# Moving the token routing and the row sends of an attention and mixture-of-experts kernel one slot later

## The reference

```python
xn = _layernorm(x, axis=-1)
x = x + attention(xn) + ffn(xn)
# attention: 16 heads of 8 numbers, causal, scores plus a decay mask, softmax, then w_proj
scores = einsum('bhqd,bhkd->bhqk', q, k) / sqrt(D) + attn_mask
y = einsum('bhqk,bhkd->bhqd', softmax(scores), v)
# ffn: 8 experts with 512 hidden numbers, the best 2 of each token
probs = softmax(einsum('btd,ed->bte', x, Wr));  topk_vals, topk_idx = top_k(probs, 2)
h = silu(einsum('btd,efd->btef', x, W1));  y = einsum('btef,edf->bted', h, W2)
out = einsum('bte,bted->btd', gate, y)
```

## Time and profile before

| | us |
|---|---|
| median of 3 runs | 507.46 (504.73 to 507.56) |
| the profiled execution: its time | 506.12 |
| the profiled execution: its span | 504.4 |
| PE busy | 478.1 |
| DVE busy | 365.7 |
| POOL busy | 366.2 |
| ACT busy | 336.6 |

### The profile page before, as it was taken

The page is one execution under the profiler, slowest core; times in us unless marked ns, Lnnn a source line. Parts: engine busy times, 40 slices in busy tenths (PEclk is TensorE's granted clock), DMA queues, the critical chain, the costliest instruction groups (busy, mean ns, idle before and its releaser), DMA issues.

```text
span 504.4 us, 13425 instructions
## 1 busy us (share of the span) xinstructions
PE 478.1 (95%) x4294; PEld 346.7 (69%) x4294; DVE 365.7 (73%) x1407; ACT 336.6 (67%) x621; POOL 366.2 (73%) x591
## 2 busy tenths in 40 slices
PE   6769899999999999999999999989999999999997
PEld 5645465555664665566566556689999999999564
DVE  7888989988999989989889897733333333333887
ACT  4789878888888888887988888752233233232762
POOL 3587987889888889889889888734454554555784
PEclk9998999999999999999999999999999999999999
DMA  6479790780470461353255153877676777672634
GB/s 188 126 278 286 201 215 16 213 199 18 133 215 28 143 182 57 122 158 102 90 159 138 51 183 112 227 223 238 199 210 208 210 208 207 191 216 69 246 118 140
DMA packets 72755, 82.24 MB, mean 163 GB/s; under 512 B 8638, under 2 KB 52704, under 8 KB 72688
## 3 DMA queue, kind: packets, MB, share of 16 engines
q1 hardware_dynamic: 68368, 72.91, 50.3%
q0 software_dynamic: 4320, 8.47, 4.7%
HBM read 49.94 MB, written 31.86 MB: 162 GB/s over the span
## 4 chain that ended last, share of the span: by engine, by line
PE 69%; DVE 17%; ACT 10%; issue 2%; DMA 1%; SPq 0%; ACTq 0%; DVEq 0%
PE psT L1498 22%; PE psT L1585 13%; PE ps L1558 12%; PE psO L1518 11%; DVE scores L1268 8%; PE ps L1470 6%; ACT probs L1008 4%; ACT scores L965 3%; PE psM L1446 2%; DVE x_all L608 2%; PE ps L1549 1%; ACT values L992 1%; DVE xt L1122 1%; DMA w_qkv<-w_attn 1%; DVE probs L1054 1%
## 5 line engine op out<-in xcount | busy, mean ns | idle before, releaser
L1268 DVE CUSTOM_DVE_ANT_0 scores<-ps,wdist 128x256 f32<-128x256 f32 (+3 forms) x512 | 217.3, 485 | 22.6 <-PE ps L1470 21.8
L1008 ACT ACTIVATE probs<-psT 128x512 f32<-128x512 f32 x320 | 173.8, 597 | 50.3 <-PE psT L1498 49.1
L875 POOL TENSOR_SCALAR scores<-scores,row_max 128x256 f32<-128x256 f32 (+3 forms) x388 | 185.3, 493 | 29.2 <-DVE row_max L1268 28.1
L1498 PE MATMUL psT<-ident,scores 128*128 128x128 f32 x1280 | 176.3, 281 | 5.7 <-ACT probs L1008 5.6
L1498 PEld LDWEIGHTS psT<-ident,scores 128*128 128x128 f32 x1280 | 137.7, 141 | 64.0 <-issue 46.3
L894 POOL DMA_INDIRECT picked_dram<-scores,row_ring x71 | 69.8, 983 | 70.0 <-DVE scores L1349 66.8
L1017 ACT ACTIVATE scores<-ps 128x512 f32<-128x512 f32 x71 | 42.3, 598 | 91.4 <-PE ps L1558 91.4
L1518 PE MATMUL psO<-probs,values 128*32 128x512 f32 (+3 forms) x1024 | 88.4, 441 | 0.0
L965 ACT ACTIVATE scores<-scores,row_max 128x512 f32<-128x512 f32 x124 | 83.0, 727 | 0.0
L1585 PE MATMUL psT<-xn_all,scores 128*128 x568 | 75.4, 276 | 1.6 <-ACT scores L1017 1.6
L1558 PE MATMUL ps<-scores,wdist 128*128 128x128 f32 x568 | 74.9, 275 | 0.6 <-DMA wdist<-w1t 0.6
(11 more groups left out here) (169 smaller groups left out, 295.3 us busy)
## 6 DMA issues: line engine op xcount, KB each, us to landing
wdist<-w1t SPq DMA_DIRECT2D x71, 256.0 KB, 3.4
k_rows<-k_dram SPq DMA_DIRECT2D x64, 96.0 KB, 3.0
q_rows<-q_dram SPq DMA_DIRECT2D x64, 96.0 KB, 2.9
row_ring<-rows_dram SPq DMA_DIRECT2D x71, 65.0 KB, 2.9
rows_dram<-row_ring SPq DMA_DIRECT2D x6, 650.0 KB, 6.3
k_dram<-k_parts SPq DMA_DIRECT2D x7, 384.0 KB, 2.4
q_dram<-q_parts SPq DMA_DIRECT2D x7, 384.0 KB, 2.6
xn_all<-picked_dram SPq DMA_DIRECT2D x4, 512.0 KB, 7.4
```

Source lines behind the costliest of these rows:

```text
L875: last = nc.gpsimd.tensor_scalar(part, part, -1.0, row_max[:, r, tile, quad:quad + 1], ALU.mult, ALU.add)
L1008: nc.scalar.activation(probs[:, at.ring(2), w, :], psT[:, w % 2], ACT.Exp, scale=-1.0).then_inc(exp_ready, 1)
L1268: last = nc.vector.tensor_tensor_reduce(out=scores[:, r, u, col:col + n], in0=bank[:, col:col + n], in1=wdist[:, at.g * QUADS + quad, SEQ ...
L1498: last = nc.tensor.transpose(psT[:, w % 2, place * P:(place + 1) * P], scores[:, at.ring(2), u, col + key * P:col + (key + 1) * P], ident[:])
```

## The change

Every entry of ROUTE moves to the next slot, so the routing stands in slots 3 to 13 in place of 2 to 12, and FIRST_SEND_SLOT is 9 in place of 8, so the sends stand in slots 9 to 28 in place of 8 to 27. SECOND_PICK_SLOT, where the second pick's places are written into the rows, follows to slot 19. The wait of R9 for the counts names slot 5, where CT now stands. Nothing is added or taken away.

```diff
-ROUTE = {2: {0: ("R1",), 1: ("R2",), 3: ("R3",)},
-         3: {0: ("R4",), 1: ("R5",), 3: ("R6",)},
-         4: {0: ("R7", "GX"), 1: ("CT",), 3: ("R8",)},
-         5: {0: ("R9",), 3: ("R10",)},
...
-         12: {0: ("R17",)}}
-FIRST_SEND_SLOT = 8
+ROUTE = {3: {0: ("R1",), 1: ("R2",), 3: ("R3",)},
+         4: {0: ("R4",), 1: ("R5",), 3: ("R6",)},
+         5: {0: ("R7", "GX"), 1: ("CT",), 3: ("R8",)},
+         6: {0: ("R9",), 3: ("R10",)},
...
+         13: {0: ("R17",)}}
+FIRST_SEND_SLOT = 9
...
-                    dve.wait_ge(misc_free, MISC["CT", 4] + 1)
+                    dve.wait_ge(misc_free, MISC["CT", 5] + 1)
```

More of the change, by code:

```diff
@@ L72 @@
 DVE_BATCHES, POOL_BATCHES = (4, 5, 6, 7), (0, 1, 2, 3)
-ROUTE = {2: {0: ("R1",), 1: ("R2",), 3: ("R3",)},
-         3: {0: ("R4",), 1: ("R5",), 3: ("R6",)},
-         4: {0: ("R7", "GX"), 1: ("CT",), 3: ("R8",)},
-         5: {0: ("R9",), 3: ("R10",)},
[L78 to L81, removed]
-         12: {0: ("R17",)}}
-FIRST_SEND_SLOT = 8
+ROUTE = {3: {0: ("R1",), 1: ("R2",), 3: ("R3",)},
+         4: {0: ("R4",), 1: ("R5",), 3: ("R6",)},
+         5: {0: ("R7", "GX"), 1: ("CT",), 3: ("R8",)},
+         6: {0: ("R9",), 3: ("R10",)},
+         7: {0: ("R11",), 3: ("R12",)},
+         8: {0: ("R13",), 3: ("R14",)},
+         9: {0: ("R15",)},
+         12: {0: ("R16",)},
+         13: {0: ("R17",)}}
+FIRST_SEND_SLOT = 9
 ALL_UNITS = UNITS * NGROUP
```

## The result

The changed kernel takes 518.32 us (median of 6 runs, 516.55 to 520.55), the kernel before 507.02 in the same comparison: a ratio of 1.0257, with an interval of 1.0226 to 1.0287 (it isn't the quotient of the two medians, which is 1.0223). By the ratio the changed kernel stands at 520.5 on that median, a little above the range of 511.5 to 520.

The account below looks back on a forecast made before the run. PE was taken to end most slots, the DVE some, and the last send's load chain to reach PE last. Early slots -0.8, sends' end +10.0 and clock +0.8 give +10.0 on 506.12; forecast 516.8 us, range 511.5 to 520.

Parts of the forecast that it names:

- The end of the sends: Hand-over to the experts: the last send starts later and PE's first up matmul moves by the whole delay, +10.0 us.
- The clock: Experts' start: after PE's idle stretch the granted clock falls to half for a while, +0.8 us, between 0 and 1.65.
- the sum of the early slots: Slots that give or receive routing, plus the XN steps: together -0.8 us, bounds about -3.5 and +3.
- The routing: Routing pieces moved one slot later: -1.0 + 0 + 1.2 + 1.0 + 0 + 0.3 us over the slots.
- Slots 2 and 6: Slot 2 loses R1 to R3, -1.0 us; slot 6 swaps R11 and R12 for R9 and R10, +1.0.
- Slot 5: It receives the counting, 2.02 us on PE, and becomes 13.2 us long with a little idle: +1.2.
- Slots 7 and 8: R13 and R14 go from slot 7 to 8; what one wins the other loses: 0, between -1 and +1.4 us.
- R16 in slot 12: Part of one term for R15 to R17, short instructions going to slots 9, 12 and 13: +0.3 us together.
- XN: Scaling of tokens on the DVE: both long cases, slots 12 and 16, become short, -2.3 us, bounds -2.4 and 0.
- rival (b): XN stays long or finds other slots, so the -2.3 falls away: 519.1 us, chance 0.13.
- Rival (a): Row tiles behind w2 issue in 1.86 us instead of 4.75, PE starts 2.9 earlier: 513.9 us, chance 0.12.
- Rival (c): Not slower: the early slots give back what the routing cost them, about 509.4 us or within 1%, chance 0.05.

Follow-up runs that it names:

- sends alone late: Kernel before with only the sends moved, to slots 9 to 28, the routing staying in slots 2 to 12: 514.57 us, ratio 1.0175.
- w1 first: Changed kernel with SP issuing four w1 ahead of its wait for the landing, then four row tiles, w2, four more row tiles: 515.22 us, ratio 1.0201.
- the kernel in which it was kept up: Changed kernel with 44 idle matmuls put in front of PE's wait for the first row tile: 521.11 us, ratio 1.0318.
- routing alone late: Changed kernel with the second pick's sends packed into slots 19 to 27, so the last send is in slot 27 as before: 509.31 us, ratio 1.0061.
- first pick's four-send slots moved, w1 first: Kernel before with those slots moved from 11 and 15 to 12 and 16, and four w1 loaded ahead of SP's wait: 508.81 us, ratio 1.0084.

## Why the prediction was right and wrong

**The end of the sends: right in its mechanism, and in its size partly by luck.** The last send starts 23.58 us into slot 27 where it was 13.50: +10.1, forecast +10.0. The prediction then kept two times of the kernel before, and both were off: from the last send to w2 it took 4.34 in place of 2.35, and w1, issued at 337.92 and used at 341.21, arrived 1.2 quicker (3.3 for 4.45). They nearly cancel; together +10.85. With the landing at 2.35 again (second pick's four-send slots moved back) the kernel is 4 us faster, 2 of them from the landing. That it was this chain is shown by the sends alone late, which have the same wait, and by w1 first, which changes only the chain.

**The clock: the size fits.** The half clock came, for longer than in the earlier trace rows. From the first up matmul to the ninth slot's the changed kernel took 0.9 us more than the kernel before, forecast 0.8, and the two other kernels with the half clock there took 0.8 and 1.5 more. That the clock alone makes this difference isn't shown: in the kernel in which it was kept up, two slower loads took as much. Behind the ninth slot the profiled execution lost another 1.2 us, 0.8 of them in two short waits near 457 us, that no part of the change explains.

**The step that failed is the sum of the early slots, -0.8.** It came out at about +1.5 (slots 2 to 28 of the profiled executions), 2.3 more than forecast, in two of its terms:

- The routing, forecast -1.0 + 0 + 1.2 + 1.0 + 0 + 0.3 = +1.5, cost +3.1 (changed kernel against sends alone late; 2.6 in the routing alone late, whose slot 6 takes 9.78). Slots 2 and 6 were right, -1.1 and +1.1. Slot 5 was +1.8 in place of +1.2; the forecast took 13.10 of PE's time and then 0.1 of idle time, and it was 0.7. Slot 3, taken as unchanged, was +0.3 and slot 4 -0.4. Slots 7 and 8 don't cancel: -0.7 and +1.3, since slot 7 ends on PE when the DVE gets lighter, while slot 8 has no PE work to hide R13 and R14 in. R16 in slot 12, forecast as 0.3, cost 0.85 (9.47 against 8.62 for sends alone late).
- XN, forecast -2.3: slots 12 to 18 of the sends alone late are 2.3 shorter than before, as forecast, and moving the four-send slots alone gives 2.1. But the prediction looked only one slot ahead: four sends in slot 22 make POOL late through slot 23, so a new long XN stands in slot 24, and slots 19 to 28 are 0.8 longer. With these four sends back in slot 21 the 0.8 is gone. This is a part of rival (b): a long XN did find another slot, but it cost 0.8 and not 2.3.

The Trainium skill (SBUF — State Buffer, Who interferes with whom) has the shut-out end with the one GpSimd instruction that came first. The runs bear out that the two exclude each other and not that it ends there: 2.97 and 2.60 us for XN, 2.10 for a copy of 0.19, beside POOL instructions of 0.46 (5.54 / 12).

Rival (a) didn't come: the row tiles behind w2 took 4.78 to issue again. Rival (c) was on the wrong side: the early slots took more, not less. The two profiled spans are 14.4 apart, the medians 11.3, and the ratio makes it 13.0: the profiled execution after is the slowest of its six, so 1 to 3 us of the parts above need not be the change's. Of the 4.4 by which the profiled execution missed the +10.0, the early slots are 2.3, the end of the sends 0.85, the clock 0.1 and the stretch behind the ninth slot 1.2.

## What to carry to other kernels

When work is moved one step later in a fixed order, look first at who waits for its last piece: here PE already waited 0.63 us for that chain, so it had no margin, and about 10 us of delay came through whole. For the rest, the price of a moved piece is read in the slot that receives it, by the engine that is last there, and slot by slot; a total of equal work is no zero. And a stall that a late engine causes has to be followed until that engine has caught up, which may be two or three slots on.

## What the runs showed of the hardware that was not expected

A DVE instruction beside a burst of POOL instructions can take until the burst's last one and not only until the end of the one that it met: 2.97 us in place of 0.78 for XN. In slot 12 of the kernel before it ended at 160.94, during the burst's last instruction (160.39 to 161.18). The long ones came at the sixth to eighth of the burst's 12 instructions and the short ones of slots 12 to 24 at the eighth or ninth, but one that came at the ninth took 2.10 (first pick's four-send slots moved, w1 first). So the place goes with the length and doesn't settle it; what lets the DVE in is open.

The landing of the last send takes about 2.35 us in some kernels and over 4 in others. The transfer view of the changed kernel from 325.0 to 329.5 (DMA busy by slices, then MB by queue) shows it:

```profile
DMA  0092000000000940000400000020000000000000
...
q0 software_dynamic: 64, 0.13, 9.5%
q8 instruction: 1, 0.02, 1.2%
```

The last send's packets are the pair of slices around 326.5, but the last two come only at 328.0 and 328.5, behind a fetch of instructions (q8) from 327.2 to 328.0; SP goes on at 329.29. The four other kernels whose last sends stand in slot 28 behind four in slot 26 have the same picture. In the kernel with the second pick's four-send slots moved back, all packets of the last send are through in one piece ahead of such a fetch, and SP goes on 2.35 us after the send's start. That the fetch holds up the two packets is read from the times alone; no run tried it. Against it: the fetch starts 2.2 us after the send here and 2.35 there, and in both the other packets are through after 1.9.
